# First loads as one list in order of need, with the groups, LayerNorm and retention of the first blocks rearranged, and the last tile written in pieces

## The chip, the cores and the metric

The kernel runs on the 8 cores of one Trainium2 chip. Each core works on two of the sixteen sequences, with the same program, and no core waits for another. A core has a matmul engine (TensorE, PE in the profile, with its weight loads as PEld), a vector engine (VectorE, DVE), an activation engine (ScalarE, ACT), GpSimd (POOL) and SyncE (SP), which here only issues transfers. The time is the device time of the slowest core in microseconds (us).

## The reference

x has 16 sequences of 2048 rows with 1024 columns. All weights are shared.

```python
xn = _layernorm(x)                       # over the 1024 columns, eps 1e-5
# retention, 4 heads: q, k of 256, v of 512 columns
q, k = apply_rotary(xn @ Wq, xn @ Wk);  v = xn @ Wv
attn = einsum(q, k) * D[rel];  o = attn @ v + (q * cross_q) @ S;  S = gC * S + (k * cross_k)^T @ v
o = rmsnorm(o, gn_weight) * silu(xn @ Wg)
s = o @ Wo                               # 2048 -> 1024
# feed-forward, 3072 hidden, integer weights times 1/127
g = silu((silu(xn @ wg.T) * (xn @ wu.T)) @ wd.T)
out = x + s * g
```

## The kernel before

A core treats its two sequences one after the other. A sequence has 16 tiles of 128 rows. Each phase works in bfloat16 with sums in PSUM.

**Start, first sequence.** The 16 x tiles are read into eight buffers xa (`xa_load`, by SP), normalised in two steps (`ln0_stats` for one tile, `ln0_chain` for several tiles at once: nine small dependent steps on DVE), scaled by `ln0_apply` on DVE or ACT, and transposed into xnT: tiles 0 to 7 on PE with an evacuation by ACT (`ln_trans_pe`), tiles 8 to 15 by a DMA transpose that SP issues (`ln0_trans`). The weights of head 0 (wqA and wkA in 2 pieces each, wvA and wgA in 4 each, read as float32 and written as bfloat16) come through POOL's queue (`w_load`). `warm` fills PE with matmuls of 256 columns whose results are not used. They wait for the constants.

**Projections.** For each of 16 pairs of head and quarter of the sequence (bi, four blocks to a head) there are 12 groups of eight matmuls: two for q, two for k, four for v, four for g. `group` takes one of four ring buffers R in PSUM, `g_qk` evacuates it with a cast on ACT and, after the second, rotates on DVE (`rope`) and, for k, has SP issue a DMA transpose into ktok. `g_vg` evacuates on ACT. A group of q or k needs four tiles of xnT, one of v or g needs one.

**Retention.** 64 chunks of 128 rows follow the projections at a distance of 12 groups: `ret.slot(p - 12)` ahead of group p. Slot 3i has the state update of chunk i (PE into U, then DVE S<-S,U, which frees U), slot 3i+1 the scores of chunk i+1 (PE into R, DVE to atm) and the gating of chunk i-1 (DVE, which waits for POOL's reciprocal root), slot 3i+2 the output of chunk i (PE into OA, a square on ACT, six small steps on POOL).

**Order.** Every engine executes its instructions in the order in which the program records them, and each waits for the semaphore counts given to it. The order of the first blocks is the list `first` in `order(0)`. What LayerNorm does between the groups of the first sequence is written in `ln0_step(p)`, where p counts the groups: statistics of tiles 8 to 11 at p = 12 to 15, their chain at 16, applications at 20 and 22; tiles 12 to 15 at p = 24, 25, 28 and 30, their chain at 31, applications at 32 and 34. Then each sequence has its feed-forward part: four blocks with 48 groups of gate and up (`gate_up`) and four tiles of `tile_out` each: 48 matmuls into U, 32 into OA, a multiply and an add on DVE over 1024 columns, and the store.

## Time and profile before

| | us |
|---|---|
| three runs | 2081.14, 2087.50, 2081.78 |
| median | 2081.78 |
| profiled execution | 2081.98 |
| its span on the slowest core (core 5) | 2080.4 |
| spans of the other cores | 2069.6 to 2076.9 |
| PE busy on core 5 | 2044.2 |
| start of the first projection group on core 5 | 22.89 |
| start of the first group with wqB on core 5 | 147.51 |

The views of the trace used below show one execution on core 5, unless another core is named. Times in a timeline row are the start from the span's begin, then the duration of the merged instructions; a bracket holds the idle time of the engine ahead of them and what ended it. The last matmul of a merged row is shown with its latency, so rows overlap a little.

### The profile page before, as it was taken

How to read it: one execution, taken by the hardware profiler on the slowest of the kernel's cores; microseconds unless marked ns; L12 is line 12 of the kernel's file. 1: busy time of each engine (PE TensorE's matmuls, PEld its weight loads, DVE VectorE, ACT ScalarE, POOL GpSimd, SP SyncE). 2: the span in 40 equal slices, each digit the busy share in tenths (PEclk: the TensorE clock that was granted, in tenths of full speed). 3: DMA queues.
4: the chain of work that ended last, by engine and by line, in shares of the span. 5: the costliest groups of instructions: out<-in, count | busy, mean ns of one | idle time of the engine just before them, and what ended most of it. 6: DMA issues, size and time to landing. Idle time of an engine off the chain costs nothing.

```text
span 2080.4 us, 28596 instructions; the slowest of 8 cores (2069.6 to 2080.4 us)
## 1 busy us (share of the span) xinstructions
PE 2044.2 (98%) x9688; PEld 936.5 (45%) x9688; DVE 696.9 (33%) x1159; ACT 497.3 (24%) x887; POOL 362.8 (17%) x996
## 2 busy tenths in 40 slices
PE   5999999999999999999999999999999999999998
PEld 3444444444444444444444444444444444444443
DVE  4564545442132231231245444544311211211211
ACT  3444443431001011011023444443210110110110
POOL 1244454444000000000103333333300000000000
PEclk9999999999999999999999999999999999999999
DMA  8457898779545455445714343434862352452432
GB/s 204 102 92 107 121 133 140 133 138 233 168 136 155 138 144 168 125 146 159 144 44 72 51 79 66 88 69 82 190 195 71 132 162 71 144 150 71 157 87 70
DMA packets 217278, 256.75 MB, mean 123 GB/s; under 512 B 136112, under 2 KB 153648, under 8 KB 217136
## 3 DMA queue, kind: packets, MB, share of 16 engines
q1 hardware_dynamic: 187184, 200.39, 34.3%
q0 software_dynamic: 29952, 54.54, 18.9%
q8 instruction: 81, 1.33, 0.3%
q14 instruction: 61, 0.50, 0.1%
HBM read 244.39 MB, written 46.14 MB: 140 GB/s over the span
## 4 chain that ended last, share of the span: by engine, by line
PE 96%; DMA 2%; DVE 1%; SPq 0%; issue 0%; ACT 0%; DVEq 0%; POOL 0%; ACTq 0%; POOLq 0%
PE R L381 63%; PE U L697 16%; PE OA L716 11%; PE OA L524 2%; PE U L492 2%; PE OA L519 1%; DMA xa<-x 1%; PE R L471 1%; DMA wqA<-wq 1%; DMA xnT<-xn 1%; SPq L202 0%; SPq L198 0%; DVE st L296 0%; ACT xn L335 0%; DVE st L297 0%
## 5 line engine op out<-in xcount | busy, mean ns | idle before, releaser
L381 PE MATMUL R<-xnT,wgu 128*128 128x512 bf16 x3072 | 667.0, 379 | 0.0
L381 PEld LDWEIGHTS R<-xnT,wgu 128*128 128x128 bf16 x3072 | 300.3, 98 | 361.1
L697 PE MATMUL U<-wd_sb,hT 128*128 128x512 bf16 x1536 | 336.7, 379 | 0.0
L669 DVE TENSOR_TENSOR hT<-sg,R 128x512 bf16<-128x512 bf16 x192 | 131.6, 687 | 492.0 <-PE R L381 490.9
L660 ACT ACTIVATE sg<-R 128x512 bf16<-128x512 f32 x192 | 114.7, 597 | 568.3 <-PE R L381 562.0
L697 PEld LDWEIGHTS U<-wd_sb,hT 128*128 128x128 bf16 x1536 | 150.3, 98 | 181.2
L716 PE MATMUL OA<-wo_sb,ogl 128*128 128x512 bf16 x1024 | 226.2, 379 | 0.0
L504 DVE SCALAR_TENSOR_TENSOR S<-S,U 128x1024 bf16<-128x1024 bf16 x112 | 136.6, 1220 | 200.3 <-PE U L492 200.3
L724 DVE TENSOR_TENSOR g<-g,OA 128x1024 f32<-128x1024 f32 x32 | 39.1, 1221 | 430.9 <-PE OA L716 430.9
L716 PEld LDWEIGHTS OA<-wo_sb,ogl 128*128 128x128 bf16 x1024 | 100.2, 98 | 120.8
L708 ACT ACTIVATE g<-U 128x1024 f32<-128x1024 f32 x32 | 32.8, 1024 | 481.7 <-PE U L697 481.7
L535 POOL TENSOR_SCALAR nr_sb<-ss_sb,sml_sb 128x1 f32<-128x1 f32 x128 | 42.4, 331 | 483.0 <-ACT dump L529 469.9
L431 ACT ACTIVATE vt<-R,sml_sb 128x512 bf16<-128x512 f32 x128 | 88.0, 688 | 159.1 <-PE R L381 159.1
L381 PE MATMUL R<-wvB,xnT 128*128 128x512 bf16 x512 | 120.1, 379 | 0.0
L381 PE MATMUL R<-wgB,xnT 128*128 128x512 bf16 x512 | 119.5, 379 | 0.0
L394 ACT CAST eraw<-R 128x512 bf16<-128x512 f32 x128 | 75.0, 586 | 174.8 <-PE R L381 128.1
L436 ACT ACTIVATE gg<-R 128x512 bf16<-128x512 f32 x128 | 76.3, 597 | 141.6 <-PE R L381 141.6
L245 POOL TENSOR_SCALAR nr_sb<-nr_sb 128x1 f32<-128x1 f32 x256 | 89.0, 348 | 45.2 <-POOL nr_sb L241 23.0
L552 DVE SCALAR_TENSOR_TENSOR og<-OA,nr_sb,gg 128x512 bf16<-128x512 f32 x128 | 94.9, 742 | 3.6 <-POOL nr_sb L248 2.9
L198 POOL DMA_DIRECT2D wqA<-wq x4 | 2.2, 544 | 490.4 <-PE R L381 476.7
L529 ACT ACTIVATE dump<-OA 128x512 bf16<-128x512 f32 x128 | 76.4, 597 | 20.3 <-PE OA L524 8.4
L248 POOL TENSOR_SCALAR nr_sb<-nr_sb 128x1 f32<-128x1 f32 x256 | 69.1, 270 | 46.3 <-POOL nr_sb L245 46.3
(87 smaller groups left out, 1652.5 us busy)
## 6 DMA issues: line engine op xcount, KB each, us to landing
wgu<-wgu_bf SPq DMA_DIRECT2D x192, 512.0 KB, 4.0
og_sp<-og SPq DMA_DIRECT2D x128, 128.0 KB, 3.8
ox<-x SPq DMA_DIRECT2D x32, 512.0 KB, 4.5
out<-ox SPq DMA_DIRECT2D x32, 512.0 KB, 3.3
wd_sb<-fdw POOLq DMA_DIRECT2D x48, 256.0 KB, 6.4
xa<-x SPq DMA_DIRECT2D x16, 512.0 KB, 17.4
xl<-x SPq DMA_DIRECT2D x16, 512.0 KB, 4.2
wgu_bf<-fgw POOLq DMA_DIRECT2D x24, 256.0 KB, 5.6
```

The source lines that it names most:

```text
L245: t = lane.do(lambda e, p=p: e.tensor_scalar(out=a, in0=p, scalar1=p, scalar2=v, op0=ALU.mult, op1=ALU.mult), sem)
L381: ins = e.matmul(ring[r][:, :], l, m, start=(k == 0), stop=(k == KC - 1))
L394: t_ev = ACT.do(lambda e: e.copy(out=eraw[:, e0:e0 + 512], in_=ring[r][:, :]), sACT)
L431: t_ev = ACT.do(lambda e: e.activation(out=dst, in_=ring[r][:, :], func=AF.Identity, scale=sml_sb[:, h:h + 1]), sACT)
L436: t_ev = ACT.do(lambda e: e.activation(out=dst, in_=ring[r][:, :], func=AF.Silu), sACT)
L504: self.st[i + 1] = DVE.do(lambda e: e.scalar_tensor_tensor(out=dst[:, :], in0=src[:, :], scalar=float(GC[h]), in1=U[:, :], op0=ALU.mult, o ...
L529: self.sq[i] = ACT.do(lambda e: e.activation(out=dump[:, :], in_=OA[:, ob:ob + 512], func=AF.Square, scale=SQRT2, accum_out=ss_sb[:, i % 4 ...
L552: self.og[i] = DVE.do(lambda e: e.scalar_tensor_tensor(out=og[:, b:b + 512], in0=OA[:, ob:ob + 512], scalar=nr_sb[:, 4 * q + 1:4 * q + 2], ...
L660: t_ev = ACT.do(lambda e: e.activation(out=sg[:, g0:g0 + 512], in_=ring[r][:, :], func=AF.Silu, scale=Q127), sACT)
L669: t_ev = DVE.do(lambda e: e.tensor_mul(out=hT[:, m * 512:(m + 1) * 512], in0=sg[:, g0:g0 + 512], in1=ring[r][:, :]), sDVE)
L697: ins = e.matmul(U[:, n * 512:(n + 1) * 512], hT[:, k * 512 + tt * 128:k * 512 + (tt + 1) * 128], wd_sb[:, k * D + n * 512:k * D + (n + 1) ...
L716: ins = e.matmul(OA[:, n * 512:(n + 1) * 512], ogl[:, (t % 2) * 2048 + k * 128:(t % 2) * 2048 + (k + 1) * 128], wo_sb[:, k * D + n * 512:k ...
```

## The change

**Loads.** The two tables of constants become one (`cst`). The first loads are written as one list: x0, x1, the constants, x2, x3, four pieces of wv, x4, x5, two of wq, cos and sin of block 0, x6, x7, two of wk, four of wg, cos and sin of block 1, x8, x9, later x10, x11, the other cos and sin, x12 to x15. `in_turn` makes each entry from the fifth on wait, on the queue that issues it (SP or POOL), until the third entry before it has landed. The constants are outside the count. Each weight piece of head 0 has a semaphore of its own, and a group that reads them waits piece by piece (`parts`).

**Start.** Warm-up is one run of 90 matmuls on a tile that DVE clears, ahead of all else on PE. The statistics of tile 2 stand inside the chain of tiles 0 and 1.

**Order of the first blocks.** The v groups of block 0, its q groups, two v groups of block 1, the k groups of block 0, the other two v groups of block 1, the g groups. The transposes of tiles 4 to 7 stand singly between them. Tiles 8 to 15 are normalised in pairs: statistics of two tiles, chain, two applications on ACT and two DMA transposes are recorded together at p = 13, 17, 25 and 29. Retention's first slots come at other steps (`late`): slot -2 at p = 15, slots 0 and 1 at 16 and 17, 2 and 3 at 18, 4 and 5 at 19, 6 and 7 at 20, 8 at 21, 9 and 10 at 22, 11 at 23. From p = 24 on it is p - 12 again.

**Last tile.** The last tile's 1024 columns are written in pieces of 512, 256 and 256, the third into ring buffer 0, each with its own multiply, add and store.

```diff
-        for o_, i_ in ((idm_sb, idm_d), (sml_sb, sml_d)):
-            t_const[0] = dma(SP, S["const"], o_[:, :], i_[:, :])
+        t_const[0] = dma(SP, S["const"], cst_sb[:, :], cst_d[:, :])
...
-    def ln0_chain(c0, m):
+    def ln0_chain(c0, m, fill=()):
...
+        for f in fill:
+            f()
...
+        for n, (k0, t_w) in enumerate(parts):
+            k1 = parts[n + 1][0] if n + 1 < len(parts) else KC
+            PE.wait(t_w)
+            tok = PE.do(lambda e, k0=k0, k1=k1: go(e, k0, k1), sPE if k1 == KC else None)
...
+        pieces = [(0, 1024, OA[:, :])]
+        if s == SEQ - 1 and t == NCH - 1:
+            PE.wait(*ring_free)
+            pieces = [(0, 512, OA[:, 0:512]), (512, 256, OA[:, 512:768]), (768, 256, ring[0][:, 0:256])]
...
-        first = [(0, v), (0, qk), (1, v), (0, g), (1, qk), (1, g)]
+        first = [(0, v), (0, qk[:2]), (1, v[:2]), (0, qk[2:]), (1, v[2:]), (0, g), (1, qk), (1, g)]
...
+    def in_turn(lane, fn):
+        if len(stream) > 3:
+            lane.wait(stream[-3])
+        stream.append(fn())
...
+    x_turn(0, 1)
+    consts()
+    x_turn(2, 3)
+    w_turn(2, 0, 1, 2, 3)
+    x_turn(4, 5)
+    w_turn(0, 0, 1)
+    cs_turn(0)
+    x_turn(6, 7)
+    w_turn(1, 0, 1)
+    w_turn(3, 0, 1, 2, 3)
+    cs_turn(1)
...
-    warm(32)
-    ln0_pair(0)
+    warm(90)
+    ln0_pair(0, [lambda: stats0(2)])
...
+        if p == 3:
+            ln0_pair(4)
+            apply0(4, False)
+            apply0(5, True)
+        elif p in (4, 5):
+            ln_trans_pe(p, ln_tok[p])
+            if p == 4:
+                ln0_pair(6)
+                apply0(6, False)
...
-        elif 12 <= p < 40:
-            t, n = 8 + 4 * (p // 12 - 1), p % 12
-            if p < 24 and n < 4 or p >= 24 and n in (0, 1, 4, 6):
-                ln0_stats(t + (n if p < 24 else (0, 1, 4, 6).index(n)))
-            elif n == (4 if p < 24 else 7):
-                ln_tok["c"] = ln0_chain(0, 4)
-            elif n in (8, 10):
-                for u in (t + n - 8, t + n - 7):
-                    apply0(u, True)
-                    ln0_trans(u, ln_tok[u])
+        elif 12 <= p < 36 and p % 12 in (1, 5):
+            t = 8 + 4 * (p // 12 - 1) + p % 12 // 2
+            ln0_pair(t)
+            for u in (t, t + 1):
+                apply0(u, True)
+                ln0_trans(u, ln_tok[u])
+
+    late = {15: (-2,), 16: (0,), 17: (1,), 18: (2, 3), 19: (4, 5), 20: (6, 7), 21: (8,), 22: (9, 10), 23: (11,)}
...
-            ret.slot(p - 12)
+            for j in late.get(p, ()) if s == 0 and p < 24 else (p - 12,):
+                ret.slot(j)
```

On PE, at the start of the program up to the first groups of g, the kernel before has this (R<-idm_sb,xn are the transposes, R<-wvA,xnT the v groups, R<-xnT,wqA and wkA the q and k groups):

```order
L739 MATMUL R<-idm_sb 128x256 x32
L353 MATMUL R<-idm_sb,xn_70 128x128 x16
L739 MATMUL R<-idm_sb 128x256 x24
L381 MATMUL R<-wvA,xnT 128x512 x8
L353 MATMUL R<-idm_sb,xn_70 128x128 x8
L381 MATMUL R<-wvA,xnT 128x512 x8
L353 MATMUL R<-idm_sb,xn_70 128x128 x8
L381 MATMUL R<-wvA,xnT 128x512 x16
L381 MATMUL R<-xnT,wqA 128x512 x16
L381 MATMUL R<-xnT,wkA 128x512 x16
L353 MATMUL R<-idm_sb,xn_70 128x128 x16
L381 MATMUL R<-wvA,xnT 128x512 x16
```

The changed kernel, on PE from the fourth v group's end (the third row holds the second q group, and the last row the g groups):

```order
L386 MATMUL R<-xnT,wqA 128x512 x8
L357 MATMUL R<-cst_sb,xn_69 128x128 x8
L386 MATMUL R<-xnT,wqA 128x512 x8
L357 MATMUL R<-cst_sb,xn_69 128x128 x8
L386 MATMUL R<-wvA,xnT 128x512 x16
L386 MATMUL R<-xnT,wkA 128x512 x8
L357 MATMUL R<-cst_sb,xn_69 128x128 x8
L386 MATMUL R<-xnT,wkA 128x512 x8
L357 MATMUL R<-cst_sb,xn_69 128x128 x8
L386 MATMUL R<-wvA,xnT 128x512 x16
L386 MATMUL R<-wgA,xnT 128x512 x24
```

The transposes of tiles 4 to 7 moved apart, and the k groups behind two v groups of the next block.

On POOL's queue, the weight pieces of head 0, before (the waits name the semaphores of x tiles):

```order
L198 DMA wvA<-wv 128x1024 x2
L198 DMA wvA<-wv 128x1024 [waits xa0]
L198 DMA wvA<-wv 128x1024
L198 DMA wqA<-wq 128x1024 [waits xa3]
L198 DMA wqA<-wq 128x1024
L198 DMA wkA<-wk 128x1024 x2
L198 DMA wgA<-wgt 128x1024 [waits xa5]
L198 DMA wgA<-wgt 128x1024 x3
```

And now (w0 and w1 are the pieces of wq, w2 and w3 of wk, w4 to w7 of wv, w8 to w11 of wg, cs0 the tables of block 0):

```order
L198 DMA wvA<-wv 128x1024 [waits xa1]
L198 DMA wvA<-wv 128x1024 [waits xa2]
L198 DMA wvA<-wv 128x1024 [waits xa3]
L198 DMA wvA<-wv 128x1024 [waits w4]
L198 DMA wqA<-wq 128x1024 [waits w7]
L198 DMA wqA<-wq 128x1024 [waits xa4]
L198 DMA wkA<-wk 128x1024 [waits cs0]
L198 DMA wkA<-wk 128x1024 [waits xa6]
L198 DMA wgA<-wgt 128x1024 [waits xa7]
L198 DMA wgA<-wgt 128x1024 [waits w2]
L198 DMA wgA<-wgt 128x1024 [waits w3]
L198 DMA wgA<-wgt 128x1024 [waits w8]
```

Every piece waits for a landing, where four pieces waited before.

On DVE, from the rotation of block 1's q (steps 17 and 18), before (S<-S,U is the state update that frees U):

```order
L408 TENSOR_TENSOR ropeA<-eraw,cos_sb 128x1024
L409 TENSOR_TENSOR ropeB<-eraw,sin_sb 128x1024
L412 TENSOR_TENSOR qT_76<-ropeA,ropeB 128x512
L414 TENSOR_TENSOR qT_76<-ropeA,ropeB 128x512
L504 SCALAR_TENSOR_TENSOR S_82<-S_81,U 128x1024
L477 SCALAR_TENSOR_TENSOR atm<-R,idm_sb 128x128
L552 SCALAR_TENSOR_TENSOR og<-OA,nr_sb,gg_75 128x512
```

And now, from the end of that rotation on, with the second tile's statistics:

```order
L423 TENSOR_TENSOR qT_75<-ropeA,ropeB 128x512
L298 BN_STATS st_93<-xa 128x6
L299 BN_STATS st_93<-xa 128x6
L301 BN_AGGR mv_94<-st_93 128x2
...
L309 TENSOR_SCALAR nl_95<-mv_94 128x2
...
L322 SCALAR_TENSOR_TENSOR nl_95<-nl_95 128x2
L325 SCALAR_TENSOR_TENSOR nl_95<-mv_94,nl_95 128x2
L513 SCALAR_TENSOR_TENSOR S_80<-S_81,U 128x1024
L486 SCALAR_TENSOR_TENSOR atm<-R,cst_sb 128x128
```

Fifteen rows of LayerNorm (two tiles' statistics and a chain) stand between the rotation and the state update now.

## Rows read from the trace of the kernel before

**Rows 1.** The page: its first line, and busy time of PE.

```profile
span 2080.4 us, 28596 instructions; the slowest of 8 cores (2069.6 to 2080.4 us)
...
PE 2044.2 (98%) x9688; PEld 936.5 (45%) x9688; DVE 696.9 (33%) x1159; ACT 497.3 (24%) x887; POOL 362.8 (17%) x996
```

**Rows 2.** Busy time by stretch: length, PE, PEld, DVE, ACT, POOL, granted clock, DMA share, GB/s.

```profile
22.90:62.10 39.20, 28.83 (x151) 13.19 (x149) 15.67 (x48) 17.41 (x22) 2.41 (x5) 0.87 0.83 206
62.10:147.50 85.40, 79.57 (x371) 35.60 (x370) 53.09 (x107) 38.70 (x69) 29.50 (x80) 0.96 0.54 86
147.50:2067.40 1919.90, 1919.90 (x9067) 877.44 (x9066) 616.99 (x978) 435.56 (x792) 326.50 (x901) 1.00 0.53 123
```

**Rows 3.** Waits of PE over the span: sum in us, times, longest.

```profile
PE R L739 <- DMA sml_sb<-sml: 14.2, 1, 14.2
...
PE R L381 <- DMA xnT<-xn: 5.8, 4, 2.6
```

**Rows 4.** Timeline of PE, 20 to 150 us: start, duration, instruction, idle before.

```profile
20.27 2.78 PE L739 MATMUL R<-idm_sb 128*128 128x256 bf16 x24
22.89 1.89 PE L381 MATMUL R<-wvA,xnT 128*128 128x512 bf16 x8
...
34.34 5.30 PE L381 MATMUL R<-xnT,wqA 128*128 128x512 bf16 x16 [2.04 <-DMA wqA<-wq]
40.29 3.61 PE L381 MATMUL R<-xnT,wkA 128*128 128x512 bf16 x16 [0.65 <-DMA wkA<-wk]
...
50.35 6.03 PE L381 MATMUL R<-wvA,xnT 128*128 128x512 bf16 x16 [5.56 <-ACT xnT L359]
...
62.10 1.89 PE L381 MATMUL R<-wgA,xnT 128*128 128x512 bf16 x8
...
147.51 1.89 PE L381 MATMUL R<-xnT,wqB 128*128 128x512 bf16 x8
```

**Rows 5.** The same two markers on core 0.

```profile
55.34 1.89 PE L381 MATMUL R<-wgA,xnT 128*128 128x512 bf16 x8
...
136.30 1.89 PE L381 MATMUL R<-xnT,wqB 128*128 128x512 bf16 x8
```

**Rows 6.** Queues in the first 50 us: packets, MB, share of 16 engines.

```profile
q1 hardware_dynamic: 3284, 7.40, 48.8%
q0 software_dynamic: 1728, 3.15, 43.7%
```

**Rows 7.** Tile 3's statistics on DVE, and landing of the xa loads.

```profile
20.56 0.69 DVE L296 BATCH_NORM_STATS2 st<-xa 128x6 f32<-128x512 f32 x1 [2.32 <-DMA xa<-x]
...
DMA to landing us min/median/max: 4.2/17.4/26.7
```

**Rows 8.** Timeline of DVE and ACT: rotation, statistics of tile 6, both applications.

```profile
40.41 0.69 DVE L408 TENSOR_TENSOR ropeA<-eraw,cos_sb 128x1024 bf16<-128x1024 bf16 x1 [9.04 <-ACT eraw L394]
...
42.49 0.69 DVE L296 BATCH_NORM_STATS2 st<-xa 128x6 f32<-128x512 f32 x1
...
48.07 1.24 ACT L335 ACTIVATE xn<-xa,nl 128x1024 bf16<-128x1024 f32 x1 [3.49 <-DVE nl L321]
48.08 0.81 DVE L330 TENSOR_SCALAR xn<-xa,mv,nl 128x1024 bf16<-128x1024 f32 x1
```

**Rows 9.** Timeline: a state update on DVE, first and last step on POOL.

```profile
67.29 0.28 POOL L535 TENSOR_SCALAR nr_sb<-ss_sb,sml_sb 128x1 f32<-128x1 f32 x1 [40.19 <-ACT dump L529]
...
68.31 1.22 DVE L504 SCALAR_TENSOR_TENSOR S<-S,U 128x1024 bf16<-128x1024 bf16 x1
...
69.56 0.27 POOL L248 TENSOR_SCALAR nr_sb<-nr_sb 128x1 f32<-128x1 f32 x1 [0.17 <-POOL nr_sb L245]
```

**Rows 10.** The last steps on DVE, and landing of the out stores.

```profile
2074.70 1.22 DVE L724 TENSOR_TENSOR g<-g,OA 128x1024 f32<-128x1024 f32 x1 [14.65 <-PE OA L716]
2076.09 1.23 DVE L727 TENSOR_TENSOR ox<-ox,g 128x1024 f32<-128x1024 f32 x1 [0.17 <-DVE g L724]
...
DMA to landing us min/median/max: 2.6/3.3/5.2
```

More of the change, by code:

```diff
@@ L376, in group, with go @@
         PE.wait(ring_free[r], *toks)
-        def go(e):
-            for k in range(KC):
+        def go(e, k0, k1):
+            for k in range(k0, k1):
                 l, m = mm(k)
@@ L390, in g_qk @@
                                   xnT[:, k * T + n * 512:k * T + (n + 1) * 512]),
-                       w_tok[(s, h, which)], *(xn_tok[(s, 4 * n + u)] for u in range(4)))
+                       *(xn_tok[(s, 4 * n + u)] for u in range(4)), parts=w_tok[(s, h, which)])
         e0 = which * 1024 + d * 512
@@ new lines, in tile_out, with sm @@
+        if s == SEQ - 1 and t == NCH - 1:
+            PE.wait(*ring_free)
+            pieces = [(0, 512, OA[:, 0:512]), (512, 256, OA[:, 512:768]), (768, 256, ring[0][:, 0:256])]
+        for c0, w, bank in pieces:
+            c1 = c0 + w
+            def sm(e, c0=c0, w=w, bank=bank):
+                for k in range(16):
+                    for c in range(0, w, 512):
+                        n = min(512, w - c)
+                        ins = e.matmul(bank[:, c:c + n],
+                                       ogl[:, (t % 2) * 2048 + k * 128:(t % 2) * 2048 + (k + 1) * 128],
+                                       wo_sb[:, k * D + c0 + c:k * D + c0 + c + n], start=(k == 0), stop=(k == 15))
+                return ins
+            t_s = PE.do(sm, sPE)
+            ogl_free[t % 2] = t_s
+            DVE.wait(t_s, t_g)
+            t_m = DVE.do(lambda e, c0=c0, c1=c1, bank=bank: e.tensor_mul(out=g2[:, c0:c1], in0=g2[:, c0:c1],
+                                                                         in1=bank), sDVE)
+            free["O", 0] = free["O", 1] = t_m
+            DVE.wait(t_m, ox_tok[t % 3])
+            t_a = DVE.do(lambda e, c0=c0, c1=c1: e.tensor_add(out=ox[t % 3][:, c0:c1], in0=ox[t % 3][:, c0:c1],
+                                                              in1=g2[:, c0:c1]), sDVE)
+            g2_free[0] = t_a
+            SP.wait(t_a)
+            row = s * T + t * 128
+            ox_free[t % 3] = dma(SP, S[f"st{t % 3}"], out_d[row:row + 128, c0:c1], ox[t % 3][:, c0:c1])
@@ L732, in tile_out @@
         return t_f, t_s
+    t_dump = DVE.do(lambda e: e.memset(dump[:, :], 0.0), sDVE)
     def warm(n):
-        PE.wait(t_const[0])
+        PE.wait(t_dump)
         for _ in range(n):
-            PE.do(lambda e: e.matmul(ring[3][:, 0:256], idm_sb[:, 0:128], idm_sb[:, :], start=True, stop=True))
+            PE.do(lambda e: e.matmul(ring[3][:, 0:256], dump[:, 0:128], dump[:, 0:256], start=True, stop=True))
     def order(s):
@@ L783, in build_nc @@
     ln_trans_pe(1, ln_tok[1])
-    warm(24)
     ln0_pair(2)
@@ L787, in build_nc @@
     apply0(3, True)
-    ln0_pair(4)
-    for t in range(8, 12):
-        xa_load(t)
-    cs_load(2)
-    cs_load(3)
-    gn_load()
+    x_turn(8, 9)
     def ln0_step(p):
```

109 lines of the change are left out of this document (48 added, 61 removed), and 1 row of the table S.

## Prediction

> **What bounds the kernel now.** I read the views from coarse to fine. The page gives PE 98% of the span, so only the remainder can move [rows 1]. The table by stretch shows where it lies [rows 2]: from 147.50 to 2067.40 us PE is busy in every microsecond at a granted clock of 1.00, and this change touches nothing in there. The loss sits in three places: before the first projection group (22.9 us), from there to 147.50 us, and after the last matmul. The waits of PE [rows 3] name two of the early ones: 14.2 us for the last constant, and 5.8 us in four waits for DMA transposes of xnT. The timeline of PE dates the others and shows the slow clock: after 2.04 us idle for wqA, sixteen matmuls took 5.30 us where sixteen others took 3.61; after 5.56 us idle for the evacuation of a transposed tile they took 6.03 [rows 4]. The granted clock of the second stretch is 0.87, of the third 0.96, and 1.00 is the level of 2.4 GHz [rows 2].
>
> Two markers cut the early stretch. Group g(0,0), the first with wgA, starts at 62.10 us, and the first with wqB at 147.51 us [rows 4]. The sixteen that took 3.61 us, the last one's 0.38 included, start 0.215 apart, so a group of eight fills 1.73. From 22.89 to 62.10 PE had twelve groups (12 x 1.73 = 20.8), six transposed tiles of about 0.45 (2.7) and 0.5 of retention, so 24.0 of 39.2 us: 15.2 lost. From 62.10 to 147.51 it had 36 groups (62.2) and of retention 12 scores of 0.11, 11 updates of 0.43 and 12 outputs of 0.65, the first 0.22 (13.5): 75.8 of work, 9.6 lost. That fits PE idle for 5.8 of 85.40 and a clock of 0.96 instead of 1, worth 3.3 [rows 2]. Core 0 had these markers at 55.34 and 136.30 us and ends at 2069.6; core 5 ends at 2080.4 and sets the time [rows 1, 5]. The difference of the ends (10.8) is that of the second marker (11.2), so I only have to forecast the second marker and the tail.
>
> **First loads.** In the first 50 us the two queues took 48.8% and 43.7% of the 16 engines [rows 6]. That is 21.9 us for 12 weight pieces, 1.82 us each, and 24.4 us for 12 x tiles and 4 cos/sin pairs, about 1.7 per x tile and 1.0 per pair. The engines were full: the order of the list decides, not the number of queues. Before, x3 came only at 20.56 us, since four weight pieces and the queue ahead shared the engines with it [rows 7]. In the new list x0 to x3 go first. Data starts about 3 us in, so x0 lands near 5.4, x1 7, x2 8.5, x3 10. Then one item follows another while three are on the way: the wv pieces end at 17.3 us, x5 20.7, wq 24.3, x7 28.6, wk 32.3, wg 39.6, x9 43.8.
>
> LayerNorm of a pair of tiles on DVE took 5.58 us (42.49 to 48.07: two times 1.6 of statistics, then nine small steps in 2.4), and an application 0.81 on DVE or 1.24 on ACT [rows 8]. With x1 at 7, statistics of three tiles and the chain end near 12.7, tile 0 is normalised at 13.5 and transposed and copied (1.0 us on ACT) at 15.1. The 90 warm-up matmuls no longer wait for a constant; at 0.109 each (24 of this width fill the 2.62 from 20.27 to 22.89 [rows 4]) they need 9.8, plus 2 to 3 for a slow start (an estimate, from the 1.7 and 2.4 of [rows 4]), and end near 13 to 14, so they delay nothing. v(0,0) starts at about 15.2 instead of 22.89 and, fed piece by piece, ends at 17.6. From there I walk the new order: transposed tile 2 after 18.4 us (x3 at 10, second chain at 17.5, application 0.8), the other v groups to 24.4, q(0) to 28.3, v(1,0) and v(1,1) to 32.2, k(0) to 36.1, v(1,2) and v(1,3) to 40.0. The slacks on this way are about 0.6 us at tile 4, 0.5 at tile 6, 0 at wk and 0.4 at wg. So g(0,0) starts at 40 with all loads on time, at 42 if they come 2 to 3 us late. I take **41** for the slowest core, against 62.10: a gain of 21.
>
> **LayerNorm of tiles 8 to 15.** This is the cost. Before, statistics stood singly between retention's steps, one chain served four tiles, and applications came 4 and 6 groups later. Now a whole pair (5.58 us, of which nothing can be interleaved) stands at steps 13, 17, 25 and 29, and both applications on ACT (2.5 us) wait for the chain ahead of the evacuations of the next groups. PE has four ring buffers, and retention's U needs DVE after each update (1.22 us [rows 9]).
> - Step 13: x9 at 43.8 ends the chain at 47.8 and the applications at 50.3; the third g group's buffer is free at 51. PE wants it for scores(1) 9.2 us after g(0,0), at 50.2. With G at 41, about 1.7 idle when x9 is a little late.
> - Step 17: DVE first ropes q(1) (0.7 for the cast on ACT, 2.1 for rope [rows 8]), then the pair 5.6, then the state update 1.2, with the gaps between them 9.8 us after q(1)'s last matmul. PE has meanwhile out(0), upd(1), k, scores(2), out(1), k: 0.65+1.73+0.76+1.73 = 4.9. It idles 4.9 ahead of upd(2). Then g(1,0) needs the first k's buffer, whose cast stands behind both applications and a square on ACT: 2.1 more.
> - Step 22: gating of chunk 0 waits for POOL's 2.5 us after that late square [rows 9], rope of k and the update stand behind it: 2.2.
> - Steps 25 and 29 by the same walk: 1.9 for the second k group's buffer, 4.6 ahead of upd(7), 1.6 for the first v buffer behind the last applications.
>
> Sum 19.0 us idle. Of the slow clock, rows of the same kind gave 1.7 and 2.4 after idle of 2.0 and 5.6 us [rows 4]; part of it falls where PE would wait anyway. I take 2; the bounds are 0 and 5. On the other side the xnT transposes of tiles 8 to 11 now have until step 24 and find the loads long done, and those of 12 to 15 are issued near 27 us into a stretch of 33: the waits on xnT (9.6 with their gaps and clock) go away. So the second marker is 41 + 75.8 + 0.5 (scores and update moved behind the first marker) + 19 + 2 = 138.3 against 147.5: **9.2 gained**.
>
> Edits with one answer: one constant load instead of two saves an issue of 0.5 us on SP that nothing waits for now, since warm-up uses a memset tile. Twelve semaphores add waits on PE that are met or are the piece's own landing. POOL waits item by item until about 37 us; the first rsqrt is wanted later than 50. SP holds x8 and x9 (waiting for wg) ahead of ktok's transpose: 39.5 instead of 39.1, wanted at 47, and x12 to x15 ahead of the xnT transposes, issued by about 54, wanted later.
>
> **Tail.** Before: multiply from 2074.70 (1.22), add (1.23), store landing about 3 (shortest 2.6), end at 2080.4: 5.7 us [rows 10]. Now only 256 columns follow the last matmul: about 0.4+0.4 with the same gaps, and a quarter of the bytes, landing no later than the 2.6: 3.7. The 32 matmuls of 256 columns cost what 16 of 512 did (0.109 against 0.216 each). Gain **2.0**, bounds 1 and 3.
>
> **Sum.** 2080.4 - 9.2 - 2.0 = 2069.2 us of span. The profiled execution took 2081.98, 1.6 beyond its span, and lies 0.2 over the median of 2081.78. So 2071.
>
> **Rivals.**
> - *The LayerNorm pairs don't stall PE*: DVE gets ahead of what I assume and the buffers hold. For it: in stretch 3 DVE was busy 53.09 of 85.4 us, so there is room on average. Against: the same form of step, a pair ahead of an application on ACT, did stall PE for 5.56 us at 50.35 on core 5, with ACT idle 3.49 for the chain [rows 4, 8]. With 3 left of the 21: 2071 - 18 = 2053.
> - *The list starves the engines.* Each load is issued only when the third before it has landed. Three on the way must cover issue, latency and landing. The shortest x load took 4.2 us from issue to landing [rows 7], so at best 1.4 to 1.6 us per item against 1.7 to 1.82 of transfer: covered, barely. With landings of 8 us under load from 8 cores, an item takes 2.7 and wg ends after 10 + 17 x 2.7 = 56; the first marker is 55, 14 later than forecast, and the time 2085, no difference that can be told. At 9.5 us (3.2 an item) wg ends at 64, the first marker is 63 and the time 2093: **slower**. It turns at a first marker of 58, a landing of about 8.5 us.
> - *The gain is real but smaller*: stalls of 25 instead of 21 and a first marker of 44. That is 7 later, 2078: no difference.
>
> The Trainium skill, "DMA: Bandwidth & Descriptors", "Rules for kernel authors", advises to issue early and wait late, which speaks against holding loads back; its "Anatomy of one DMA" puts about 2.0 us of fixed cost on each transfer, mostly completion. If a third of that were lost on each of 17 items, that page's figure would make an estimate of 11 us later for the first marker and a time near 2082. The trace has no stretch with a capped list, so no row here decides it; with full engines [rows 6] the other two would fill the gap.
>
> **How the numbers follow.** A measurement tells about 0.3% (6.2 us) from no change: below 2075.5 is faster, above 2088 slower. Chances: my forecast (2065 to 2076) 0.55; pairs without stalls (2048 to 2062) 0.19; smaller gain or a half-starved list (2076 to 2088) 0.20; starved list (over 2088) 0.06. Nearly all of the first and the second are faster: 0.72; same 0.22; slower 0.06. The range leaves out the low end of the second and the high end of the third: 2052 to 2080.
>
> **What would show it.** v(0,0) at 15 to 16 us and the first wgA group at 40 to 42 on every core; x3 landed near 10. Waits of PE of 4 to 5 us ahead of a U update and 2 us ahead of the first g(1) group, released by DVE and ACT, near 57 to 64 us, and again near 105. First wqB group near 138 on the slowest core, and the cores closer together. From the last multiply's start to the end 3.7 us. A first wgA group beyond 50 says that the list starves; no wait on S or on a cast says that the walk through steps 17 and 29 is wrong.

## Result, and the profile after

Over 20 executions each, the changed kernel took a median of 2087.08 us and the kernel before 2084.07: a ratio of 1.0015, with a 95% interval from 1.0008 to 1.0022. It is slower, by less than the 0.3% that I called no change. The forecast was 2071, and the range ended at 2080: it does not hold the time. The profiled execution took 2089.39 us, its slowest core 2087.8.

Eight cores scatter by some 5 us around their middle, so below I also give the **core median**: the median span of all cores of all executions, without cores whose mean granted clock was under 0.99, a slower state that either kernel can fall into. It is 2076.6 before and 2080.5 after.

The page of the changed kernel, its first line and the busy time of PE (the answer to [rows 1]):

```profile
span 2087.8 us, 28767 instructions; the slowest of 8 cores (2075.6 to 2087.8 us)
...
PE 2054.7 (98%) x9738; PEld 943.0 (45%) x9738; DVE 700.1 (34%) x1177; ACT 495.6 (24%) x886; POOL 363.5 (17%) x996
```

The same core, 7, by stretch, with the columns of [rows 2]: from v(0,0) to the first wgA group, from there to the first wqB group, and on to 2076.30.

```profile
17.26:50.00 32.74, 26.96 (x144) 12.69 (x145) 16.46 (x48) 16.77 (x21) 4.22 (x8) 0.90 0.83 162
50.00:150.40 100.40, 83.78 (x376) 36.51 (x375) 54.37 (x120) 38.35 (x69) 30.42 (x80) 0.92 0.63 118
150.40:2076.30 1925.90, 1921.88 (x9062) 877.65 (x9061) 617.30 (x978) 435.34 (x792) 326.41 (x901) 1.00 0.54 123
```

The first stretch begins 5.6 us earlier than before (17.26 against 22.89) and is 6.5 us shorter. The second is 15.0 us longer than the 85.40 of [rows 2]. The third, where I had said that nothing changes, has 4.0 us of idle PE (1925.90 less 1921.88). The waits of PE on this core, in the form of [rows 3]:

```profile
PE U L501 <- DVE S L513: 10.2, 2, 5.4
PE R L386 <- DMA wqA<-wq: 4.8, 1, 4.8
PE U L501 <- DMA ktok<-kT: 4.0, 1, 4.0
PE R L386 <- ACT eraw L403: 2.9, 2, 1.5
PE R L480 <- ACT gg L445: 2.6, 1, 2.6
PE R L765 <- DVE dump L759: 1.9, 1, 1.9
```

The constant's wait of 14.2 us and the xnT waits of 5.8 us are gone. In their place stand the state S, a weight piece, the transposed keys and two evictions on ACT. The timeline of PE dates them (the answer to [rows 4]):

```profile
17.26 1.02 PE L386 MATMUL R<-wvA,xnT 128*128 128x512 bf16 x4 [0.91 <-ACT xnT L363]
...
32.50 1.87 PE L386 MATMUL R<-xnT,wqA 128*128 128x512 bf16 x4 [4.83 <-DMA wqA<-wq]
...
35.01 3.49 PE L386 MATMUL R<-xnT,wqA 128*128 128x512 bf16 x8
...
62.01 0.28 PE L480 MATMUL R<-qT,kT 128*128 128x128 bf16 x2 [2.62 <-ACT gg L445]
62.13 3.56 PE L386 MATMUL R<-xnT,wqA 128*128 128x512 bf16 x8
...
75.35 0.60 PE L501 MATMUL U<-vt,ktok 128*128 128x512 bf16 x2 [4.79 <-DVE S L513]
77.70 3.57 PE L386 MATMUL R<-wgA,xnT 128*128 128x512 bf16 x8 [1.53 <-ACT eraw L403]
...
115.10 1.01 PE L501 MATMUL U<-vt,ktok 128*128 128x512 bf16 x2 [5.44 <-DVE S L513]
116.98 3.45 PE L386 MATMUL R<-wgA,xnT 128*128 128x512 bf16 x8 [0.86 <-ACT vt L440]
...
150.39 1.89 PE L386 MATMUL R<-xnT,wqB 128*128 128x512 bf16 x8
...
305.31 1.01 PE L501 MATMUL U<-vt,ktok 128*128 128x512 bf16 x2 [4.01 <-DMA ktok<-kT]
```

Groups of eight that take 1.89 us elsewhere took 3.45 to 3.57 right behind an idle stretch: the granted clock of the first two stretches is 0.90 and 0.92. The queues in the first 50 us (the answer to [rows 6]), and the share of the DMA engines in the 40 equal slices of that window, 1.25 us each, in tenths:

```profile
DMA  0499999793698999799505999815999999559998
...
q0 software_dynamic: 1728, 3.15, 46.2%
q1 hardware_dynamic: 1942, 5.08, 34.7%
```

Before, the two queues filled 92.5% of that time; now they fill 80.9%, and the share falls to 0 and 0.1 near 26 and 33 us. The gaps lie early: between 3 and 40 us the share is 0.83 to 0.91 on the eight cores, where they were full before (1.02 to 1.04). The tail, the answer to [rows 10]:

```profile
2084.67 0.42 DVE L746 TENSOR_TENSOR g<-g,R 128x256 f32<-128x256 f32 x1 [0.80 <-PE R L739]
2085.20 0.43 DVE L750 TENSOR_TENSOR ox<-ox,g 128x256 f32<-128x256 f32 x1
```

From the last multiply's start to the end are 3.1 us, where it was 5.7.

### The profile page after: what moved, and what is told of

It reads as the page before. It is cut to its first block, busy times and chain, and to the rows that moved or that the text cites. A ratio compares the mean times of both kernels' runs of the same rounds, so it can differ in the third digit from the quotient of the medians.

```text
span 2087.8 us, 28767 instructions; the slowest of 8 cores (2075.6 to 2087.8 us)
## 1 busy us (share of the span) xinstructions
PE 2054.7 (98%) x9738; PEld 943.0 (45%) x9738; DVE 700.1 (34%) x1177; ACT 495.6 (24%) x886; POOL 363.5 (17%) x996
## 4 chain that ended last, share of the span: by engine, by line
PE 96%; DMA 2%; DVE 1%; issue 0%; ACT 0%; POOL 0%; SPq 0%; DVEq 0%; ACTq 0%; POOLq 0%
PE R L386 62%; PE U L712 16%; PE OA L739 11%; PE OA L533 2%; PE U L501 2%; PE OA L528 1%; DMA ktok<-kT 1%; DMA xa<-x 1%; PE R L480 1%; DMA wqA<-wq 0%; DMA wvA<-wv 0%; ACT xn L339 0%; DVE st L298 0%; DVE st L299 0%; PE R L357 0%
## 5 line engine op out<-in xcount | busy, mean ns | idle before, releaser
L739 PE MATMUL OA<-wo_sb,ogl 128*128 128x512 bf16 (+1 forms) x1024 | 224.5, 377 | 0.0
L746 DVE TENSOR_TENSOR g<-g,OA 128x1024 f32<-128x1024 f32 (+2 forms) x33 | 39.0, 1181 | 427.4 <-PE OA L739 427.3
L723 ACT ACTIVATE g<-U 128x1024 f32<-128x1024 f32 x32 | 32.8, 1024 | 481.7 <-PE U L712 481.7
L544 POOL TENSOR_SCALAR nr_sb<-ss_sb,cst_sb 128x1 f32<-128x1 f32 x128 | 42.9, 335 | 476.7 <-ACT dump L538 472.3
L440 ACT ACTIVATE vt<-R,cst_sb 128x512 bf16<-128x512 f32 x128 | 87.8, 687 | 148.0 <-PE R L386 146.2
L561 DVE SCALAR_TENSOR_TENSOR og<-OA,nr_sb,gg 128x512 bf16<-128x512 f32 x128 | 95.1, 743 | 8.8 <-POOL nr_sb L249 8.3
L246 POOL TENSOR_SCALAR nr_sb<-nr_sb 128x1 f32<-128x1 f32 x256 | 89.6, 350 | 46.1 <-POOL nr_sb L249 23.1
L501 PE MATMUL U<-vt,ktok 128*128 128x512 bf16 x240 | 72.2, 383 | 14.2 <-DVE S L513 10.2
```

Source lines behind the costliest of these rows:

```text
L246: t = lane.do(lambda e, p=p: e.tensor_scalar(out=a, in0=p, scalar1=p, scalar2=v, op0=ALU.mult, op1=ALU.mult), sem)
L440: t_ev = ACT.do(lambda e: e.activation(out=dst, in_=ring[r][:, :], func=AF.Identity, scale=sml_sb[:, h:h + 1]), sACT)
L501: ins = e.matmul(U[:, d * 512:(d + 1) * 512], ktok[:, b + d * 512:b + d * 512 + 128], vt[:, cc * 512:(cc + 1) * 512], start=True, stop=True)
L561: self.og[i] = DVE.do(lambda e: e.scalar_tensor_tensor(out=og[:, b:b + 512], in0=OA[:, ob:ob + 512], scalar=nr_sb[:, 4 * q + 1:4 * q + 2], ...
L739: ins = e.matmul(bank[:, c:c + n], ogl[:, (t % 2) * 2048 + k * 128:(t % 2) * 2048 + (k + 1) * 128], wo_sb[:, k * D + c0 + c:k * D + c0 + c ...
```

## Experiments

The markers are those of the prediction: the start of the first wgA group and of the first wqB group, as the median of the eight cores of the profiled execution. The ratio is to the kernel before, run beside it on the same chip. "Limit" is the number of loads on the way; "even" slots are one piece of the retention a step, "uneven" are those of the change. Every row but the first and e7 has the new tail.

| kernel | limit | slots | LayerNorm 8-15 | wgA | wqB | core median | ratio (95%) |
|---|---|---|---|---|---|---|---|
| before | none, old list | even | single | 56.4 | 141.7 | 2076.6 | 1 |
| changed | 3 | uneven | pairs | 47.5 | 149.4 | 2080.5 | 1.0015 (1.0008-1.0022) |
| e4 tail alone | old list | even | single | 57.1 | 142.3 | 2073.4 | 0.9984 (0.9975-0.9993) |
| e7 pairs alone, no tail | old list | even | pairs | 57.3 | 152.5 | 2086.7 | 1.0044 (1.0027-1.0061) |
| e13 | 3 | even | single | 55.4 | 138.9 | 2070.5 | 0.9974 (0.9963-0.9984) |
| e14 | 6 | even | single | 51.3 | 133.8 | 2065.1 | 0.9964 (0.9948-0.9979) |
| e2 | 3 | uneven | single | 47.5 | 141.3 | 2069.9 | 0.9985 (0.9952-1.0018) |
| e3 | 6 | uneven | single | 46.5 | 133.6 | 2064.5 | 0.9936 (0.992-0.9952) |
| e6 | 3, then 6 | uneven | single | 48.4 | 135.9 | 2066.2 | 0.9943 (0.9928-0.9958) |
| e1 | 6 | uneven | pairs | 46.8 | 143.2 | 2077.8 | 1.0006 (0.9978-1.0033) |
| e5 | 3, then 6 | uneven | pairs | 47.9 | 143.9 | 2076.5 | 1.002 (0.9985-1.0055) |
| e12 | none | uneven | pairs | 47.6 | 144.3 | 2076.2 | 0.9994 (0.9983-1.0006) |
| e8 | 3 | even | pairs | 54.3 | 151.3 | 2083.8 | 1.0051 (1.0021-1.0081) |
| e9 casts later | 3 | uneven | pairs | 47.8 | 149.4 | 2080.8 | 0.9997 (0.997-1.0023) |
| e10 | 6 | uneven | single, earlier | 46.5 | 126.3 | 2058.1 | 0.9906 (0.9877-0.9935) |
| e11 = e10 + e9 | 6 | uneven | single, earlier | 46.2 | 126.6 | 2058.1 | 0.9895 (0.9873-0.9917) |

### Each part alone: tail and pairs

**e4_tail_only** is the kernel before with the changed tail:

```diff
+        pieces = [(0, 1024, OA[:, :])]
+        if s == SEQ - 1 and t == NCH - 1:
+            PE.wait(*ring_free)
+            pieces = [(0, 512, OA[:, 0:512]), (512, 256, OA[:, 512:768]), (768, 256, ring[0][:, 0:256])]
```

> The kernel before with the last tile in pieces alone. From the last multiply's start to the end it takes 3.1 us as in the changed kernel's profile instead of 5.7: 2.0 to 3.0 us faster than the kernel before, ratio 0.9986 to 0.9990. Rival (the store's landing takes the gain back, or the narrow matmuls cost it): within 1 us.

Measured 2080.32 against 2083.45, a core median 3.2 us lower. The tail gives slightly more than the 2 to 3 us expected.

**e2_single_statistics** puts the LayerNorm of tiles 8 to 15 back in the changed kernel:

```diff
-        elif 12 <= p < 36 and p % 12 in (1, 5):
-            ln0_pair(t)
+        elif 12 <= p < 40:
+            if p < 24 and n < 4 or p >= 24 and n in (0, 1, 4, 6):
+                ln0_stats(t + (n if p < 24 else (0, 1, 4, 6).index(n)))
+            elif n == (4 if p < 24 else 7):
+                ln_tok["c"] = ln0_chain(0, 4)
...
```

> The changed kernel with LayerNorm of tiles 8 to 15 as in the kernel before (statistics singly, one chain for four tiles, applications later); loads, first blocks and tail as changed. Theory (the pairs on DVE and the applications ahead of ACT's evacuations stall PE): the waits of U for S (10.2 us), for casts (2.9) and for vt (0.9) go away with their slow clock, waits for xnT of up to 5 us come back, and the time falls by 10 to 16 us to 2071-2077. Rival (the DVE work itself is the limit, wherever it stands): the waits of U for S keep over half their length and the time stays above 2082.

The core median falls from 2080.5 to 2069.9, by 10.6 us, and the longest wait for S falls from 5.4 to 0.7 us. But the waits for transposed tiles come back larger than the 5 us expected: 5.5 to 11.5 us for the longest on each core. The timeline of PE on core 0 shows one:

```profile
93.18 3.57 PE L386 MATMUL R<-xnT,wqA 128*128 128x512 bf16 x8 [10.50 <-DMA xnT<-xn]
```

So this run doesn't show the whole price of the pairs: without them PE runs into late tiles. **e7_pairs_on_before** is the reverse, the pairs in the kernel before:

> The kernel before, with only the LayerNorm of tiles 8 to 15 changed to four pairs in steps 13, 17, 25 and 29. Loads, slots and tail as before. Theory: the pairs themselves stall the multiply (10.2 us for the state S and 2.5 us for eraw in every changed trace, gone where the single statistics came back): the stretch from the first wgA to the first wqB group grows from 85 to 95 to 98 us, and the time by 9 to 12, to about 2093. Rival: the stalls came from the late x tiles of the list and not from the pairs; then the stretch stays under 88 and the time within 3 us of before.

It took 2093.96 against 2083.19. The distance between the markers went from a median of 84.7 to 95.1 us, the core median up by 10.1. The waits of PE on core 2 show the same two releasers as the changed kernel does, beside the old ones of the start:

```profile
PE R L739 <- DMA sml_sb<-sml: 13.6, 1, 13.6
PE U L492 <- DVE S L504: 9.0, 2, 5.4
...
PE R L381 <- ACT eraw L394: 2.5, 2, 1.4
PE R L381 <- ACT gg L436: 1.2, 1, 1.2
```

So the pairs cost 10 us with the old loads too, and the late tiles of the new list are not what makes them dear. The rows of the table give their price in every setting: 10.1 (e7), 10.6 (e2), 10.3 with three-then-six (e6 to e5), and 13.3 with six on the way (e3 to e1) or with even slots (e13 to e8).

### The list and its limit

**e1_six_on_the_way**:

```diff
-        if len(stream) > 3:
-            lane.wait(stream[-3])
+        if len(stream) > 6:
+            lane.wait(stream[-6])
```

> The changed kernel with six loads on the way instead of three. Theory (the limit of three starves the DMA engines, seen as DMA shares of 0 to 0.3 near 26 us on core 7): the first wgA group starts at 42 to 45 us instead of 44.9 to 50.0, the wait of scores(1) for the third g group's buffer falls from 2.5-3.8 to under 2, and the time falls by 4 to 7 us to 2080-2083. Rival (the engines are held up by HBM or by the mixture of loads, not by the limit): the first wgA group stays within 1 us of the changed kernel's on the median core, and the time within 2 us of 2087.

**e3_six_and_single** is e1 and e2 together.

> Both edits. If both theories hold the gains add up: 2066 to 2072. If only the LayerNorm theory holds: as the run with single statistics alone, 2071 to 2077. If the early loads are not what the second stretch waits for, six on the way brings the first wgA group forward but the second marker (first wqB group) stays.

Six instead of three is worth 2.7 us with pairs and 5.4 with single statistics. The ratio of e3, 0.9936, is 2070 us, so the two gains add up as expected. The time of e1, 2082.81, is in the theory's range. What I had not expected is its first marker, 46.8, where the rival had it: as good as unchanged. The timeline on core 0 of e1 shows why, first DVE's statistics of tile 2, then PE:

```profile
15.42 0.69 DVE L298 BATCH_NORM_STATS2 st<-xa 128x6 f32<-128x512 f32 x1 [5.45 <-DMA xa<-x]
...
19.71 1.87 PE L357 MATMUL R<-cst_sb,xn 128*128 128x128 bf16 x16 [5.79 <-DVE xn L334]
22.08 2.42 PE L386 MATMUL R<-wvA,xnT 128*128 128x512 bf16 x8 [0.50 <-ACT xnT L363]
...
46.48 5.34 PE L386 MATMUL R<-wgA,xnT 128*128 128x512 bf16 x24
```

v(0,0) begins about as late as before the change. Weight pieces now go out beside the x tiles, x2 comes late, and DVE waits 5.45 us for it in the middle of the chain of tiles 0 and 1, because the change puts its statistics there. On the eight cores this wait is 4.3 to 6.2 us in e1, 3.6 to 5.4 with no limit (e12), and 0.5 to 2.1 with three. No run leaves tile 2's statistics out of the chain, so what that part of the change costs is not shown; it is the untested way to an earlier v(0,0) with full engines. Behind v(0,0) no load is waited for, and the first wgA group follows after 24.4 us: 12 groups of 1.73 and six tiles of 0.45 make 23.5, and a slow group (2.42 us for 1.89) and a wait of 0.31 us on DVE are the rest. With a limit of three v(0,0) begins at 17, but pieces come late behind it. **e5_three_then_six** was to have both:

```diff
+        d = 3 if len(stream) < 8 else 6
+        if len(stream) > d:
+            lane.wait(stream[-d])
```

> The changed kernel, with three loads on the way for the first eight items of the list (four x tiles, four wv pieces) and six from the ninth on. LayerNorm pairs, slots and tail as changed. Theory: three on the way leave the DMA engines idle between landings once the list runs (the multiply waits 7 us in pieces between 17.2 and 49.3 on core 0), and six from the start let the first two x tiles share the engines with weights (v(0,0) at 22.1 instead of 17.2, and no wait behind it); 17.2 plus the 24.4 us that the multiplies take without a wait give the first wgA group at 42 to 44, where both other limits gave 46 to 49, and 3 to 4 us less than six throughout gave: about 2078. Rival: what is loaded before that group sets it whatever the limit; then it stays at 46 to 47 and the time at 2082.

The rival had the mechanism right: 47.9, and 2083.78 us instead of its 2082. The timeline of PE on core 2:

```profile
16.76 0.59 PE L386 MATMUL R<-wvA,xnT 128*128 128x512 bf16 x2 [0.91 <-ACT xnT L363]
20.21 0.82 PE L386 MATMUL R<-wvA,xnT 128*128 128x512 bf16 x2 [2.85 <-DMA wvA<-wv]
22.79 1.01 PE L386 MATMUL R<-wvA,xnT 128*128 128x512 bf16 x2 [1.77 <-DMA wvA<-wv]
23.98 1.01 PE L386 MATMUL R<-wvA,xnT 128*128 128x512 bf16 x2 [0.18 <-DMA wvA<-wv]
...
47.67 4.70 PE L386 MATMUL R<-wgA,xnT 128*128 128x512 bf16 x21
```

The group starts at 16.76 and waits for its last pieces until 23.98; then no wait follows. x4 and x5 wait only for x2 and x3 in this form, so they overtake the last wv piece. **e6_three_then_six_single** is the same with single statistics:

> As three-then-six, and the LayerNorm of tiles 8 to 15 as in the kernel before (one tile's statistics a step, one chain for four tiles), so that the pairs are gone. Theory: both gains add. From the first wgA group at 42 to 44, the first wqB group 85 to 87 us later as with six and single statistics, at 128 to 131; about 3 us under six-and-single, so about 2066. Rival: the transposes of tiles 8 to 11, for which the multiply waited 5.5 us at 81 with six and single statistics, come no earlier when the multiplies do, and that wait grows by the 3 us; then 2069.

Its core median is 2066.2, no better than e3 (2064.5), and its second marker is 135.9 instead of the theory's 128 to 131. **e12_no_limit** has the list's order and no limit (`> 99`):

> The changed kernel (pairs, slots and tail as changed), with no limit at all on the loads on the way: the list sets the order on each queue alone. Theory, after three, six, and three-then-six all gave the first wgA group at 46.7 to 47.9: the limit only chooses between a late first tile and a late last piece of wv; without one v(0,0) starts at 24 or later, since x and weights share the engines evenly from the start, no wait follows, and the first wgA group comes at 24 plus 24.4, at 48 to 50; the time is 2083 to 2086. Rival: the limit costs more than it brings, and 45 or less comes out, with 2079.

v(0,0) began at 20.9 to 22.1 and the first wgA group at 47.6. The core median is 2076.2, 4.3 below the changed kernel. Between 3 and 40 us the DMA share is 1.01 to 1.03, and 0.96 to 1.01 in e1. The theory was right about the start, too late by 2 to 3 us about v(0,0), and too high for the time. The limit of three costs 2.7 to 5.4 us against six, three-then-six or none, and brings nothing.

With the pairs and the uneven slots this cost does not show at the first marker. It shows behind it: from marker to marker it is 101.2 us with three, and 95.8 to 96.6 with six, three-then-six and none. With three, x8 and x9 are issued only at 47.6 us on core 7, since the wg pieces go first; their statistics, the chain and the applications hold up ACT's eviction of gg, and PE waits 2.6 us for it at 62.01 (2.5 to 3.8 on the eight cores). No core of e1 has that wait. With single statistics and even slots it is otherwise: there six instead of three moves the first marker itself, from 55.4 to 51.3 (e13, e14).

### Slots

**e8_even_slots** is the changed kernel with

```diff
-            for j in late.get(p, ()) if s == 0 and p < 24 else (p - 12,):
+            for j in (p - 12,):
```

> The changed kernel, with the retention's pieces of steps 12 to 23 put back to one for each step (piece p-12 behind group p). Loads, pairs and tail as changed. Theory: the uneven slots were not what the time went into; the stretch between the first wgA and the first wqB group stays at 100 to 102 us and the time within 3 us of the changed kernel. Rival: two pieces in each of steps 18, 19 and 20 put the update of S behind the pair's statistics, and with even slots the 5 us wait at step 17 or the 2.6 us wait for gg goes; then 4 to 6 us less.

Neither was right: 3.3 us *slower* by the core median, and the first marker at 54.3 instead of 47.5. The second marker is 1.9 later (151.3); the rest of the 3.3 lies behind it and was not traced. The timeline of PE on core 2:

```profile
47.65 0.37 PE L480 MATMUL R<-qT,kT 128*128 128x128 bf16 x2 [2.97 <-DVE kT L423]
...
55.61 0.59 PE L501 MATMUL U<-vt,ktok 128*128 128x512 bf16 x2 [2.85 <-DMA ktok<-kT]
56.04 1.24 PE L386 MATMUL R<-wgA,xnT 128*128 128x512 bf16 x5
```

With even slots retention's first pieces stand ahead of the wgA groups and wait for the rotated and then for the transposed keys, 5.8 us. The uneven slots put them behind. So most of the marker's move had a reason that is not the loads. And of the 6.8 us that the uneven slots win there 5.0 are lost again: from marker to marker it is 96.2 us with even slots and 101.2 with uneven ones, and the wait for gg (2.5 to 3.8 us) is 1.2 us or less in e8. The last two runs part the start from the slots, without the pairs.

> The kernel before with the list (three on the way) and the tail in pieces only: single statistics for tiles 8 to 15 and one piece of the retention a step, as before. It is the single-statistics kernel with even slots. Core median of that one: 2069.9; of the kernel before with the tail alone: 2073.4. Theory: the slots bring 3 us of what list and slots brought together (even slots cost 3.0 on the changed kernel), so the list of three brings almost nothing of its own: core median 2072 to 2074, though v(0,0) begins 5 us earlier. Rival: slots and pairs act on each other, and the slots are worth nothing without the pairs: then 2070.

> The same with six on the way. Theory: the limit of three takes back most of what the order of the list brings; with six the list alone gives what six-and-single gave less the 3 us of the slots: core median 2067 to 2068, 5 us under the list of three. Rival: with even slots the first pieces of the retention wait for the rotated keys whatever the loads do, and six is worth 2 us or less over three: 2070 to 2072.

e13: 2070.5, the rival's value; the slots are worth 0.6 us without the pairs (2070.5 to 2069.9, and 2065.1 to 2064.5 with six). They bring the first marker 7.9 us forward (55.4 to 47.5), and PE then waits for the transposed tiles 8 to 11, up to 11.5 us in e2 and at most 2.6 in e13. e14: 5.4 under e13, as the theory said, and 2 to 3 below the level it gave, because it still counted 3 for the slots. The new start with its limit of three brings 2.9 us, the same with six 8.3. "New start" is the list together with the warm-up, the one table of constants, tile 2's statistics in the first chain and the new order of the first blocks; no run parts these.

### The wait near 300 us

On cores 1, 4, 6 and 7 of the changed kernel PE waits 2 to 4 us for the transposed keys near 303 to 305 us, and the distance from the first wqB to the first wgu group is 305.4 to 310.3 us instead of 303.2. SP's row for the transpose on core 7 in its timeline:

```profile
287.49 2.56 SPq L202 DMA_TRANSPOSE ktok<-kT  x1
```

The landing times of this tile's 32 transposes on that core:

```profile
DMA to landing us min/median/max: 3.0/4.5/17.6
```

The 17.6 is this one. Beside it POOL issues the weights of head 3 and casts of FFN weights. **e9_later_casts** moves six of these casts:

```diff
-    pace(0, 32, 37, pieces[26:32])
-    pace(0, 46, 61, pieces[32:48])
+    pace(0, 46, 61, pieces[26:48])
```

> The changed kernel, with the six casts of FFN weights that POOL issues between pieces 32 and 37 of the retention (near 270 to 300 us, beside the loads of head 3's weights) moved to pieces 46 to 61, with the casts that are there already. Nothing else. Theory: the wait of 2 to 4 us for the transposed keys (ktok) near 300 us, on four of eight cores of the changed kernel, comes from a transfer queue that is full there; with less beside it the wait goes, the stretch from the first wqB to the first wgu group is 303 to 304 us on every core, and the slowest core, and with it the time, is 3 to 5 us shorter: about 2083. Rival: the loads of head 3 and the stores of og alone make the wait, or it is of another origin; then it stays on three to five cores, at 306 to 311, and the time at 2087.

The distance is now 303.2 to 303.9 on seven cores and 305.1 on one, and 304.7 at most in e11, which has the same move; each of the two kernels that differ from them in the casts alone (changed and e10) has cores at 307.1 to 310.3. So most of the wait came with these casts. But the time went down by little: the casts, later now, are waited for themselves, as the waits on core 4 show, and the core median is 2080.8. The median of the slowest core fell from 2085.4 to 2083.8.

```profile
PE U L501 <- DVE S L513: 9.7, 3, 5.4
PE R L386 <- DMA wgu<-wgu_bf: 4.0, 3, 1.7
```

That the wait is rarer in the kernel before (one core of eight, 1.3 us) isn't explained. It is not the loads at the start: e7, which has the old list and the pairs, shows distances of 307 to 310 on six cores; e4, with neither, 304.1 at most; the kernels with the new list and single statistics in their old places, over 305 on one or two cores each. That stays open.

### A version that beats both

In e3 one large wait is left, 4.4 to 6.4 us on the eight cores; on core 6 it ends at 80.85 us. The applications of tiles 8 to 11, and with them their transposes, stand behind groups 20 and 22:

```profile
80.85 3.57 PE L386 MATMUL R<-xnT,wqA 128*128 128x512 bf16 x8 [5.47 <-DMA xnT<-xn]
```

**e10_six_early_transposes**:

```diff
-            elif n in (8, 10):
-                for u in (t + n - 8, t + n - 7):
+            elif n in ((6, 8) if p < 24 else (8, 10)):
+                k = n - (6 if p < 24 else 8)
+                for u in (t + k, t + k + 1):
```

> As six-and-single (six on the way, single statistics, the tail in pieces, the uneven slots), with the applies and transposes of tiles 8 to 11 behind groups 18 and 20 instead of 20 and 22. Theory: the 5.3 to 5.5 us for which the multiply waits at 81 for the transposed tiles is the transposes' place behind groups 20 and 22; two groups (3.5 us) earlier takes 3.5 of it: the stretch between the first wgA and the first wqB group goes from 86.4 to 83, and the time from 2069.5 to about 2066. Rival: the applies then stand ahead of gate and eraw evictions that the multiply waits for, and what is gained at 81 is lost at 65; then 86 and 2069.

**e11_six_early_later_casts** adds e9's move:

> As six with early transposes, and the six casts moved to pieces 46 to 61. Theory: both act as they do alone: 83 us between the first two marks, no wait for ktok near 290, so that the slowest core stands 3 to 4 us above the median one less than without: about 2063. Rival: as for the casts alone, 2066.

Core medians of 2058.1 for both, 6.4 below e3, where I had expected 3.5: the longest wait for transposed tiles is down to 1.2 to 1.5 us, and the slow clock behind it (3.57 us for the group) is gone. On core 5 of e10 the granted clock from marker to marker (46.3 to 125.2) is 1.00 and PE is busy for 76.86 of 78.90 us:

```profile
46.30:125.20 78.90, 76.86 (x375) 35.35 (x374) 52.83 (x107) 38.75 (x69) 29.83 (x80) 1.00 0.74 143
```

e11 took 2062.65 us (2061.12 to 2063.37) where the kernel before took 2085.28 beside it, by the ratio 1.05% less. What the casts add to e10 is not told apart: the core medians are equal.

## Why the prediction was wrong, step by step

**The sum, on the slowest core.** Forecast span 2069.2, measured 2087.8, 18.6 more: first marker 50.0 instead of 41 (+9.0), from there to the second 100.4 instead of 97.3 (+3.1), from the second to the first wgu group 310.3 instead of 303.2 (+7.1), tail 3.1 instead of 3.7 (-0.6).

**First marker: the step that failed.** I wrote "The engines were full: the order of the list decides" and let one item follow another at 1.82 and 1.7 us while the list also kept its order. The runs show one or the other. With the order enforced (three on the way) v(0,0) began at 16.4 to 17.4 but the engines stood idle in between: on core 7 the first of the 17 items from wv to wg was issued at 7.65 us and the last at 42.72, which is 2.19 from one to the next. With full engines (six or none) x2 came late, and v(0,0) began at 21 to 23. Both ways the marker is near 47. On core 7 the 9.0 us are: v(0,0) 2.1 late (17.26 for 15.2); idle of 5.8 in the stretch, against 2.3 in my walk (25.8 less 23.5 of work); and 3.5 of slow clock (26.96 busy less 23.5), which I had not counted there at all. Of the idle 4.83 was for wqA, on this core alone (0.6 at most on the others, where pieces of wv cost 1.9 to 4.2 and of wk up to 3.6). Most of the 2.1 comes from x2, which I had landing at 8.5: DVE waits for it in the middle of the first chain, since the change puts its statistics there.

```profile
11.00 0.69 DVE L298 BATCH_NORM_STATS2 st<-xa 128x6 f32<-128x512 f32 x1 [1.72 <-DMA xa<-x]
```

The rival "the list starves the engines" had the mechanism: by its rule, a third of a landing for each item, the landings measured (medians of 5.5 to 7.0 us for the five kinds of loads) give 1.8 to 2.3 us an item, and 2.19 it was. I took it to need landings of 8.5 us to matter, since I priced it alone; at 6 us it was already enough to spoil a sum in which nothing else had been left over. The result lies at the upper end of the case "smaller gain or a half-starved list", to which I gave 0.20.

The Trainium skill, "DMA: Bandwidth & Descriptors", section "Rules for kernel authors", says to issue early and to wait late, and here it was the better guide: dropping the limit took 4.3 us off the core median (e12). The estimate of 2082, which I had made from the fixed cost of some 2 us for a transfer in the Trainium skill, section "Anatomy of one DMA" of the same page (a figure for transfers that GpSimd issues, as it does for 12 of the 17 items), ended nearer than my sum. By the Trainium skill, same page, section "Queues, rings and completion order", each engine takes turns between the queues at the grain of a packet. The traces agree: without a limit the first piece of wv is issued at 1.55 us and DVE waits for x2 until 14.54 on core 0, with three at 7.18 and until 10.92.

**The base of the comparison: the second failure.** I set 41 against core 5's 62.1 and 138.3 against its 147.5, and called the difference of 9.2 the gain. But core 5 was the late one of that execution; the medians are 56.4 and 141.7. Against these the same 138.3 is a gain of 3.4. My walk has no term for the scatter of the cores, so it is one of a middle core, and the slowest stands some 5 us above that, before as after (2081.7 over 2076.6, 2085.4 over 2080.5). Done so, my own steps would have given 2069.2 + 5 + 1.6, some 2076. That is still 11 below what was measured, and of these 6.5 are the first marker (47.5 for 41) and 3.9 the distance (101.2 for 97.3).

**The marker itself.** Of the 8.9 us by which the median first marker moved, 6.8 came back when the slots were made even (e8). I had taken the marker for a measure of the loads. The second marker, where list and single statistics with even slots gave 138.9 against 141.7 (e13), is the honest one: 2.8.

**LayerNorm pairs: right in place and kind, near in size.** I had 4.9 ahead of upd(2), measured 4.79 at 75.35; 2.1 for the cast behind it, 1.53 at 77.70; 4.6 ahead of upd(7), 5.44 at 115.10; 1.6 for the v buffer, 0.86 at 116.98; 1.9 for the second k buffer, 1.37 at 101.41; 1.7 at step 13, 2.62 at 62.01. The 2.2 of step 22 did not come. Idle 16.6 us (100.40 less 83.78) against 19.0. The rival "the pairs don't stall PE" is refuted by e2 and e7.

**Clock: mis-sized.** I took 2, bounded by 5. The work in this stretch is 75.8 + 0.5; PE was busy 83.78 us, so the slow clock cost 7.5 on core 7, against 3.8 before by the same working (79.57 less 75.8). My rows had single idle stretches of 2.0 and 5.6 us; here six waits stand in one stretch, and three of them were followed by a group that took 3.45 to 3.57 us instead of 1.89, one by an update of 1.01 instead of 0.59.

**Behind the second marker.** "This change touches nothing in there" was true of the program and false of the time: four cores waited for ktok near 300 us.

**Tail.** 2.0 forecast, 2.6 on the trace, 3.2 by e4, just over the upper bound of 3.

**What each part is worth**, by core medians in a chain from 2076.6: tail -3.2, new start with a limit of three -2.9, slots -0.6, pairs +10.6, which is 2080.5. The parts act on each other, so another chain shares them out otherwise: with the pairs in, the slots are worth -3.3, and with even slots the pairs cost 13.3. My sum had about +12 for the pairs, -2 for the tail and -21 for the start.

## What to carry to other kernels

Compare stretches by the median core, never by the one that happened to be slowest, and check that a marker does not move with an edit other than the one that it is to measure. A list of loads can be kept in order by waiting for earlier ones only at the price of gaps; count either full engines or a kept order, not both. On an engine that others wait for (DVE here), spread a block of small steps between the consumers' pieces: the same work in four blocks of 5.6 us cost 10 to 13 us, and with single statistics and early applications (e10) the longest waits between the markers were 0.7 us for S and 1.5 for transposed tiles. And a step that brings work forward pays only if what the work needs next comes forward too: with single statistics the slots moved the first marker by 7.9 us and the end by 0.6. Moving the applications too (e10) brought another 6.4, though no run moves them with even slots.
